# 35 of the 1563 chunks of a graph layer are fetched row by row from SyncE instead of gathered by GpSimd

## What is computed

```
seg  = dst * R + edge_type                       # R = 65
sums = segment_sum(x[src], seg)                  # the gather of 200000 rows
agg  = sums / max(count(seg), 1)                 # [N, R, 128]
conv = einsum('nri,rio->no', agg, W_rel) + x @ W_root + bias
h    = conv + x @ W_res + b_res
h    = batchnorm(h) * gamma + beta ; h = relu(h)
out  = layernorm(x + h)
```

## Time and profile before

| | |
|---|---|
| Median of 3 runs | 2438.82 us |
| The profiled execution | 2435.85 us, span 2434.1 us |
| Mean granted TensorE clock | 0.927 |
| DMA | 235.05 MB, mean 97 GB/s; GpSimd's queue 204.97 MB, 37.8% of 16 engines |
| Gathers | 1563 |

### The profile page before, as it was taken

How to read it: one execution, slowest core, us unless ns; L and a number is a source line. 1 busy time by engine, 2 the same in 40 slices (tenths; PEclk the granted TensorE clock), 3 DMA queues, 4 the chain that set the end, 5 groups by cost and what they waited for, 6 DMA issues and landing times.

```text
span 2434.1 us, 38062 instructions
## 1 busy us (share of the span) xinstructions
PE 2068.4 (85%) x13324; PEld 1930.0 (79%) x13324; DVE 1349.3 (55%) x2517; ACT 1458.8 (60%) x1626; POOL 1496.9 (61%) x1581
## 2 busy tenths in 40 slices
PE   3789888889888888888888898888989888988997
PEld 1588878878788778888888787888878877877887
DVE  4655556546546546546556555555545555554655
ACT  2466665666666566665666665656666566666664
POOL 3466666666666666666666666666666666666640
PEclk8999899989999899999999989999998999999999
DMA  8444444444433443444434443444444443444333
GB/s 278 112 105 91 94 90 90 95 89 90 96 89 89 95 91 88 94 89 90 96 89 90 89 96 88 89 97 89 89 95 90 91 91 89 89 91 90 90 72 107
DMA packets 246738, 235.05 MB, mean 97 GB/s; under 512 B 27081, under 2 KB 241779, under 8 KB 245907
## 3 DMA queue, kind: packets, MB, share of 16 engines
q0 software_dynamic: 225072, 204.97, 37.8%
q1 hardware_dynamic: 21475, 27.60, 3.6%
HBM read 219.66 MB, written 12.80 MB: 95 GB/s over the span
## 4 chain that ended last, share of the span: by engine, by line
PE 72%; ACT 10%; issue 9%; another core or an unknown queue 4%; DVE 3%; DMA 1%; ACTq 1%; SPq 0%; POOL 0%; DVEq 0%; POOLq 0%
PE tb L588 36%; PE ps L558 21%; ACT agg L671 10%; PE ps L564 9%; PE tb L504 4%; DVE onehot L868 1%; DVE same L810 1%; PE tb L545 1%; ACTq L671 0%; PE tb L546 0%; DMA xtab<-agg 0%; DMA xg<-xtab,srcT 0%; DVE lst L1051 0%; ACT xT L679 0%
## 5 line engine op out<-in xcount | busy, mean ns | idle before, releaser
L469 POOL DMA_INDIRECT xg<-xtab,srcT x1563 | 1492.7, 955 | 862.0 <-issue 378.2
L671 ACT ACTIVATE agg<-ps 128x390 f32 (+1 forms) x1563 | 1426.6, 921 | 926.7 <-PE ps L564 443.2
L868 DVE TENSOR_SCALAR onehot<-iota,segT,vT 128x456 fp32r<-128x456 f32 x1563 | 1084.9, 742 | 705.5 <-PE ps L564 467.9
L588 PE MATMUL tb<-agg,wsb 128*128 128x144 f32 x6370 | 1244.8, 320 | 216.9 <-issue 152.2
L588 PEld LDWEIGHTS tb<-agg,wsb 128*128 128x128 f32 x6370 | 945.6, 203 | 240.0 <-issue 174.8
L558 PE MATMUL ps<-onehot,xg 128*128 128x390 f32 (+1 forms) x3126 | 1030.1, 412 | 57.7 <-issue 37.2
L558 PEld LDWEIGHTS ps<-onehot,xg 128*128 128x128 f32 x3126 | 536.0, 202 | 107.6 <-issue 79.1
L564 PEld LDWEIGHTS ps<-onehot,xg 128*128 128x128 f32 x2930 | 573.8, 201 | 52.5 <-issue 48.6
L564 PE MATMUL ps<-onehot,xg 128*128 128x66 f32 x2930 | 474.9, 242 | 32.8 <-issue 31.8
L504 PE MATMUL tb<-same,identb 128*128 128x512 bf16 x416 | 108.4, 384 | 24.5 <-DVE same L810 21.5
L889 DVE SCALAR_TENSOR_TENSOR tmph<-iota,lastg,tb 128x72 f32<-128x72 f32 x98 | 28.1, 286 | 178.8 <-remote 168.7
(11 more groups left out here) (112 smaller groups left out, 317.9 us busy)
## 6 DMA issues: line engine op xcount, KB each, us to landing
xg<-xtab,srcT POOLq DMA_INDIRECT x1563
xtab<-agg SPq DMA_DIRECT2D x4, 1536.0 KB
hinit<-H SPq DMA_DIRECT2D x1, 3125.0 KB
agg<-in_x_dram SPq DMA_DIRECT2D x4, 768.0 KB, 7.2
out_dram<-agg SPq DMA_DIRECT2D x6, 448.0 KB, 3.5
dsth<-in_dst_dram SPq DMA_DIRECT2D x23, 64.0 KB
eth<-in_edge_type_dram SPq DMA_DIRECT2D x23, 64.0 KB
srcr<-in_src_dram SPq DMA_DIRECT2D x12, 64.0 KB
```

Source lines behind the costliest of these rows:

```text
L469: pool.indirect_dma_start(out=xg[c % RING][:], out_offset=None, in_=xtab.bitcast(F32R), in_offset=bass.IndirectOffsetOnAxis(ap=srcT[t % 2] ...
L588: ins = nc.tensor.matmul(o, wsb[:, r * F:(r + 1) * F], pair_rhs(p, r), start=(r == 0), stop=(r == R - 1))
L671: nc.scalar.activation(agg_group(g)[:, bass.ds(off, n), :], ps[c % NPS][:, 0:n * R].rearrange("f (n r) -> f n r", r=R), ACT.Copy).then_inc ...
L868: nc.vector.tensor_scalar(onehot[o][:].rearrange("p (a b) -> p a b", a=3), iota3[:, :, 0:IW], segT[t % 2][:, k:k + 1], vT[t % 2][:, k:k + ...
```

## The change

In each tile the chunks k = 28, 70 and 112 are no longer gathered by GpSimd, from chunk 50 on: 35 chunks. For each SyncE copies the chunk's 128 source numbers into one partition (`snum`, two buffers), loads them into registers, four at a time, and issues one DMA per row from `xtab` into `xf` (three buffers, fp32), whose address comes from the register. ScalarE copies `xf` into the one buffer `xs` of type fp32r, six chunks ahead of the chunk that uses it. TensorE waits for that copy in place of the gather, and reads `xs`. GpSimd's ring of 18 counts its own gathers only. The row loads of tile t+1, for t from 1 on, are issued behind the gather of the first such chunk of tile t, and `hinit` behind the first gather.

```diff
--- before.py
+++ after.py
@@ -24,6 +24,10 @@
 RING = 18
 NOH = 10
 NPS = 6
+SP_MARKS = (28, 70, 112)
+SP_FIRST = 50
+NSX = 3
+XS_AHEAD = 6
 CMAX = 12
 PE_CMP = 70
 DVE_CMP = 76
@@ -37,6 +41,7 @@
 DVE_OFFS = 122
 SCALE = 27720.0
 EPS = 1e-5
+NODES = "the sources are numbers of nodes"
 CLAMPED = "the offsets are clamped to the aggregation region when they are made"
 
 
@@ -94,6 +99,10 @@
     def last_of_group(c):
         return c % GC == GC - 1 or c == NCH - 1
 
+    by_sp = [c for c in range(SP_FIRST, NCH - 1) if c % TC in SP_MARKS]
+    by_pool = [c for c in range(NCH) if c not in by_sp]
+    turn_of = {c: n for n, c in enumerate(by_pool)} | {c: n for n, c in enumerate(by_sp)}
+
     def pair_len(p):
         return min(2 * GC, NCH - p * 2 * GC)
 
@@ -114,6 +123,9 @@
         agg = sb("agg", [P, 2 * PREG], F32)
         H = sb("H", [P, N + WIN], F32)
         xg = [sb(f"xg{s}", [P, 2 * F], F32R) for s in range(RING)]
+        xf = [sb(f"xf{s}", [P, 2 * F], F32) for s in range(NSX)]
+        xs = sb("xs", [P, 2 * F], F32R)
+        snum = [sb(f"snum{s}", [1, P], I32) for s in range(2)]
         onehot = [sb(f"onehot{s}", [P, OW], F32R) for s in range(NOH)]
         srcr = sb("srcr", [P, P], I32)
         dsth = sb("dsth", [P, HW], I32)
@@ -235,6 +247,9 @@
         offs_rdy = sem("offs_rdy")
         oh_rdy = sem("oh_rdy")
         gath = [sem(f"gath{s}") for s in range(RING)]
+        sgath = [sem(f"sgath{s}") for s in range(NSX)]
+        snum_in = [sem(f"snum_in{s}") for s in range(2)]
+        xs_rdy = sem("xs_rdy")
         agg_ps = sem("agg_ps")
         evac = sem("evac")
         root_tr = sem("root_tr")
@@ -318,6 +333,9 @@
             one_chunk(NCH - 1, ELAST)
 
         GMM = ceil_div(R, 4)
+
+        def rows_in_sbuf(c):
+            return xs if c in by_sp else xg[turn_of[c] % RING]
 
         def agg_group(g):
 
@@ -377,12 +395,41 @@
                 sp.dma_start(col(c), colvec(a)).then_inc(small_in, 16)
             sp.dma_start(wsb[:].rearrange("p (r f) -> p r f", f=F), w_rel.rearrange("r p f -> p r f")).then_inc(w_in, 16)
 
-            for t in range(1, NTL):
-                sp.wait_ge(raw_free, t)
-                load_rows(t)
-                if t == 1:
+            def numbers(n):
+                c = by_sp[n]
+                sp.dma_start(snum[n % 2][:], src[c * P:(c + 1) * P].rearrange("(a e) -> a e", a=1)
+                             ).then_inc(snum_in[n % 2], 16)
+
+            def gather_rows(n):
+                s = n % NSX
+                if n >= NSX:
+                    sp.wait_ge(xs_rdy, n - NSX + 1)
+                sp.wait_ge(snum_in[n % 2], 16 * (n // 2 + 1))
+                for q in range(0, P, 4):
+                    nodes = nc.values_load_multi_w_load_instructions(
+                        snum[n % 2][0:1, q:q + 4], engines=[ENG.SP], min_val=0, max_val=N - 1,
+                        skip_runtime_bounds_check_because=NODES)[1]
+                    for i in range(4):
+                        sp.dma_start(xf[s][q + i:q + i + 1, :], xtab[bass.ds(nodes[i], 1), :]
+                                     ).then_inc(sgath[s], 16)
+
+            sp.wait_ge(raw_free, 1)
+            load_rows(1)
+            numbers(0)
+            sp.wait_ge(tab_out, 16 * 5)
+            loaded = 1
+            for n, c in enumerate(by_sp):
+                if n + 1 < len(by_sp):
+                    numbers(n + 1)
+                gather_rows(n)
+                if n == 0:
                     sp.wait_ge(root_h, NROOT)
                     sp.dma_start(hinit, H[:, 0:N]).then_inc(hinit_out, 16)
+                if c // TC == loaded and loaded + 1 < NTL:
+                    loaded += 1
+                    sp.wait_ge(raw_free, loaded)
+                    load_rows(loaded)
+            assert loaded == NTL - 1
 
             def fast():
                 pass
@@ -460,15 +507,15 @@
             nc.gpsimd.memset(rest, 0.0).then_inc(consts, 1)
 
             pool.wait_ge(tab_out, 16 * 5)
-            for c in range(NCH):
+            for n, c in enumerate(by_pool):
                 t, k = c // TC, c % TC
                 if k == 0:
                     pool.wait_ge(colsT_rdy, t + 1)
-                if c >= RING:
-                    pool.wait_ge(agg_ps, c - RING + 2)
+                if n >= RING:
+                    pool.wait_ge(agg_ps, by_pool[n - RING] + 2)
                 pool.indirect_dma_start(
-                    out=xg[c % RING][:], out_offset=None, in_=xtab.bitcast(F32R),
-                    in_offset=bass.IndirectOffsetOnAxis(ap=srcT[t % 2][:, k:k + 1], axis=0)).then_inc(gath[c % RING], 16)
+                    out=xg[n % RING][:], out_offset=None, in_=xtab.bitcast(F32R),
+                    in_offset=bass.IndirectOffsetOnAxis(ap=srcT[t % 2][:, k:k + 1], axis=0)).then_inc(gath[n % RING], 16)
 
             def fast():
                 pass
@@ -546,21 +593,24 @@
                 nc.tensor.matmul(tb[1][:, 0:n * P], wres[:], xT[:, 0:n * P], start=False, stop=True).then_inc(root_ps, 1)
 
             def aggregate(c):
-                s, o = c % RING, c % NOH
-                pe.wait_ge(gath[s], 16 * (c // RING + 1))
+                n, o = turn_of[c], c % NOH
+                if c in by_sp:
+                    pe.wait_ge(xs_rdy, n + 1)
+                else:
+                    pe.wait_ge(gath[n % RING], 16 * (n // RING + 1))
                 pe.wait_ge(oh_rdy, c + 1)
                 if c >= NPS:
                     pe.wait_ge(evac, c - NPS + 1)
                 w = OW if last_of_group(c) else W6
                 carried = c % GC > 0
                 for part in range(2):
-                    rows = xg[s][:, part * F:(part + 1) * F]
+                    rows = rows_in_sbuf(c)[:, part * F:(part + 1) * F]
                     ins = nc.tensor.matmul(ps[c % NPS][:, 0:w], rows, onehot[o][:, 0:w], start=(part == 0),
                                            stop=(part == 1 and not carried))
                 if carried:
-                    s, o = (c - 1) % RING, (c - 1) % NOH
+                    o = (c - 1) % NOH
                     for part in range(2):
-                        rows = xg[s][:, part * F:(part + 1) * F]
+                        rows = rows_in_sbuf(c - 1)[:, part * F:(part + 1) * F]
                         ins = nc.tensor.matmul(ps[c % NPS][:, 0:R + 1], rows, onehot[o][:, W6:W6 + R + 1], start=False,
                                                stop=(part == 1))
                 ins.then_inc(agg_ps, 1)
@@ -671,6 +721,12 @@
                 nc.scalar.activation(agg_group(g)[:, bass.ds(off, n), :],
                                      ps[c % NPS][:, 0:n * R].rearrange("f (n r) -> f n r", r=R), ACT.Copy).then_inc(evac, 1)
 
+            def round_rows(n):
+                act.wait_ge(sgath[n % NSX], 16 * P * (n // NSX + 1))
+                if n >= 1:
+                    act.wait_ge(agg_ps, by_sp[n - 1] + 2)
+                nc.scalar.activation(xs[:], xf[n % NSX][:], ACT.Copy).then_inc(xs_rdy, 1)
+
             def root_copy(b):
                 n = 4 if b < NROOT - 1 else 1
                 act.wait_ge(root_tr, b + 1)
@@ -698,6 +754,8 @@
                 if c == 2 * GC:
                     act.wait_ge(root_tr, NROOT)
                 evacuate(c, offs[c % 4])
+                if c + XS_AHEAD in by_sp:
+                    round_rows(turn_of[c + XS_AHEAD])
                 if c < 2 * GC and c % 2 == 1 and c // 2 < NROOT:
                     root_copy(c // 2)
```

## The result

The changed kernel took 3299.5 us (median of 4 runs, 3296.7 to 3314.3), the kernel before 2438.5 (4 runs) beside it: ratio 1.354, 95% interval 1.351 to 1.358. Forecast were 2662 us and a range up to 2950. The sign and the place of the loss were right, the size was not. The granted clock is 0.813 on average (0.927 before), lower, as forecast for that case.

What follows compares the result with a forecast made beforehand. TensorE and its exchange with ScalarE were taken to bound the kernel before; after the change, SyncE's chain: 370.5 + 33 x 69.3 = 2657.5 us of span, with 4 added 2662 us. Range 2425 to 2950 us.

Steps and rivals of the forecast that it cites:

- SyncE is one sequencer and late: Likeliest case, chance 0.43: SyncE's sets take 63 to 78 us without overlap, delaying VectorE or ScalarE; centre 2662 us.
- the chain of row loads: Row loads behind SyncE's sets delay VectorE's first step on the last tile to 86 + 33 S; end 370.5 + 33 S.
- the size of S: SyncE's time for one chunk's numbers, register work and 128 row copies: 69.3 us, low end 60.3, high end 84.0.
- row copy: SyncE's copy of one row from the table: 0.36 us, low end 0.29, high end 0.475, 128 per chunk.
- register work: SyncE's address arithmetic: one register operation of 0.09 us with its pause per row, 11.5 us per chunk.
- register load: SyncE's load of four source numbers into registers: 0.35 us with its pause, from ScalarE's price, 32 per chunk.
- the bursts: TensorE completes chunks in bursts; the prediction said the profile doesn't show why and gave this no cost.
- The case of S above 78: Rival, chance 0.12: SyncE's row copy costs 0.475 us, S is 84.0 us and the kernel takes 3147 us.
- I took 35 gathers off at nothing: GpSimd's 35 gathers, 43.6 us, lie wholly beside TensorE's work, so removing them gains nothing.
- GpSimd was the pace: Rival, chance 0.13 wholly or in part: gathers set the time, so 44 us fewer give 2395 us if SyncE keeps up.
- the roundings: ScalarE's 35 copies of 0.40 us, 0.58 with pause, hide in its idle time: cost 0, at most 20 us.
- hinit's move: On SyncE hinit leaves at about 126 us instead of 113, before VectorE's first addition at 167: about 0.

Runs made afterwards that it cites:

- d1: The changed kernel, unaltered, on a chip of the second kind: 2788.2 us, ratio 1.333 to the kernel before there.
- a3: The changed kernel with SyncE fetching rows for the first of the 35 chunks only, ScalarE still rounding 35 times: 2388.3 us, ratio 0.979.
- a4: The changed kernel with one row fetch and one rounding for all 35 chunks: 2392.2 us, ratio 0.981.
- b1: The kernel before with GpSimd gathering only the first 18 chunks: 1914.4 us, ratio 0.785.
- e2: The changed kernel with 189 chunks not gathered, sharing one row fetch and one rounding, on a first-kind chip: 2235.8 us, ratio 0.903 to the kernel before.
- b4: The kernel before with each gather from chunk 18 on fetching 64 rows instead of 128: 2438.4 us, ratio 1.000.
- a2: The changed kernel with row copies from fixed table addresses, without register loads and register addresses: 2433.0 us, ratio 0.998.
- c2: The kernel before with buffers xf, xs and snum allocated but unused, on a second-kind chip: 2093.0 us, ratio 1.000.
- b2: The changed kernel with GpSimd gathering only its first 18 chunks, SyncE still fetching its 35, run once: 2785.5 us.
- a1: The changed kernel with two chunks per tile over SyncE instead of three, 23 in all: 2536.2 us, ratio 1.039 to the kernel before.
- c4: The changed kernel with 11 chunks over SyncE instead of 35, on a second-kind chip: 2079.4 us, ratio 0.994 to the kernel before.

## Why the prediction was wrong

**Right: SyncE is one sequencer and late, and where it shows.** Both waits are there, and the chain of row loads holds. From 59.6 us on SyncE goes from set to set; 86 + 33 S with S = 88.2 us (33 sets from 59.6 to 2994.3 us, less 24 us of row loads) gives 2997 us for VectorE's step on the last tile, and it starts at 2998.2. As S is measured on that same stretch, this confirms the order of the chain and its short links, not the size. What follows took 296.7 us instead of the 284.5 taken.

**The step that failed is the size of S, the time for one set: 69.3 us taken, 88.2 measured.** 33 x 18.9 = 624 us of the 637 missed, the longer tail the other 12. By its terms, as steps from start to start in d1, where nothing stalls:
- row copy: 0.36 taken, 0.28 measured, below my low end. The copy of one row is cheaper than the 0.36 us of 26 rows.
- register work: 0.09 taken, 0.13 measured. It is two instructions for a row, not one.
- register load: 0.35 taken from ScalarE, 0.59 measured. SyncE's own row of 0.566, set aside because it might hold a wait, was its price.
- together 128 x 0.28 + 128 x 0.13 + 32 x 0.59 = 71 us, with the numbers and longer loads 74: errors of 10 us down and 13 us up all but cancel. With it alone 370.5 + 33 x 74 + 4 = 2817 us, inside the range.
- the stalls: 14 us a set, not in the sum at all. This term took it out of the range: 33 x 14.2 = 469 us.

The trace of before held a sign of it: TensorE's 303 us of "issue". The prediction said of the bursts that it couldn't read why they came, and went on as if they couldn't touch SyncE. A sum of undisturbed durations was laid on a sequencer that would work beside the very gathers that stall another one.

**The case of S above 78 came nearest, for the wrong reason.** It gave 3147 us at 84.0, from a row copy of 0.475 us; but the copy is the one term that took less than its price, 0.28. By the rule of the Trainium skill ("DMA: Bandwidth & Descriptors", section "Why a DMA increments its semaphore by 16 and not by 1") that stood beside it, a row might be split over 16 engines. The trace shows two packets for a row: the queue has 30505 in the page of after, and before

```profile
q1 hardware_dynamic: 21475, 27.60, 3.6%
```

9030 more for 4480 row copies and 35 copies of numbers, two for each. The page's count of packets under 512 B (31036, before 27081) fits one such small packet and one whole row per copy. The row isn't split, and its price wasn't paid.

**GpSimd.** I took 35 gathers off at nothing because GpSimd stood at the end of its ring and TensorE had waited twice for a gather. a3, a4, b1 and e2 refute that: 35 gathers fewer take 46 to 50 us off, 189 fewer 239 us, and without gathers 1914 us are left. The rival "GpSimd was the pace" was right in price (2395 forecast, 2388 and 2392 measured). Its reason is only in part borne out: on the first kind of chip the gathers cost time through TensorE's stalls and clock, while GpSimd stands at the end of its ring; only on the second kind is GpSimd itself the bound. In the changed kernel the gain lies behind SyncE's lateness. The Trainium skill's rule that DMAs started from several engines save only the issue time (same page, section "Issuing engines are not separate DMA queues") I read as speaking against the change, since that time was a waiting engine's. The runs show that leaving out 35 gathers was worth 46 to 50 us all the same, and b4, with half the bytes and the same time, that it isn't the moving of the rows.

**Right at nothing:** the roundings (a3 against a4; 435 ns each in a3, 400 taken). hinit's move didn't show; VectorE's first addition of the transform (before: the earlier trace rows) is at the same place:

```profile
L947 DVE SCALAR_TENSOR_TENSOR tmph<-iota,lastg,tb x98: 277/285/293, 166.5 to 3256.9; 128x72 f32<-128x72 f32 x98
```

**Left open:** how the gathers stall the sequencers of TensorE and SyncE, why on some chips only, and why a gather costs its full step there although GpSimd is at the end of its ring. What the 45 us of a2 against a3 are wasn't split further either. And no run with 11 sets fell on a chip of the first kind, so whether that kernel gains there too isn't known.

## What to carry over

Before work goes to an idle queue, sum what its sequencer executes per row, address registers and loads included, priced by rows of that same engine, and compare the sum with the time between two deliveries. Here it was 74 us against 63, so the change had to lose even without a stall (ratio 1.333 in d1); with 11 chunks instead of 35 it gained 0.6% on the same kind of chip. Idle time named "issue" on the engine that seems to be the bound is a finding and not a remainder: take the suspected cause away once (here the gathers: 2439 to 1914 us) before anything beside it is costed at nothing. And work of an engine that waits at the end of its ring can still cost time; leave out a tenth of that work and measure.

## What the hardware showed unexpectedly

- Gathers on GpSimd stall the sequencers of other engines in pieces of about 0.7 us, on some chips: TensorE's unexplained waits in three lines are 303 us with gathers, 8 without (b1) and 11 on the other kind of chip (c2); SyncE's set with its share of row loads is 88 us against 74 (b2, d1), and the set alone 97 us where GpSimd gathers all the time (a1).
- The same program takes 2438 to 2475 us on the chips of the first kind and 2093 on those of the second, run after run, with a granted clock of 0.927 and 0.991 in the profiles at 2434 and 2093 us. On the first kind the ratio of the change is 1.354, on the second 1.333.
- An indirect gather of 64 rows takes GpSimd nearly as long as one of 128 (0.896 us against 0.941), and the kernel the same time: 2438.4 us against 2439.2.
- Some 4400 copies of one row, from another engine's queue and at fixed addresses, cost 41 to 45 us beside the gathers on the first kind of chip (a2 against a4 and a3). On the second kind 1408 of them cost next to nothing, by the estimate at c4.
